# Attention weighing of the first four key tiles cut into two halves of the queries

## The reference, cut to what matters

```python
k = _layernorm(k, kln_w, kln_b)
q = _layernorm(q, qln_w, qln_b)
dot = jnp.einsum('bqhs,bkhs->bhqk', q, k) * scale
dot = jnp.where(causal, dot, -jnp.inf)
attn = jax.nn.softmax(dot, axis=-1)
out = jnp.einsum('bhqk,bkhs->bqhs', attn, v).reshape(b, t, e)
```

## Time and profile before

| what | value |
|---|---|
| median of three runs | 3361.61 us (3357.04 to 3369.52) |
| profiled execution, first to last instruction (span) | 3276.4 us |
| PE busy in the span | 2931.8 us (89%) |
| attention's 16 groups, 99.27 to 872.90 us | 773.63 us |
| PE busy in these | 682.38 us |
| granted TensorE clock in these | 0.72 |
| granted TensorE clock over the span | 0.891 |

### The profile page before, as it was taken

How to read it: one execution, slowest core, us unless ns; L and a number is a source line. 1 busy time by engine, 2 the same in 40 slices (tenths; PEclk the granted TensorE clock), 3 DMA queues, 4 the chain that set the end, 5 groups by cost and what they waited for, 6 DMA issues and landing times. The chain is left out here.

```text
span 3276.4 us, 55735 instructions
## 1 busy us (share of the span) xinstructions
PE 2931.8 (89%) x18642; PEld 1710.9 (52%) x18643; DVE 1759.5 (54%) x3206; ACT 1418.6 (43%) x2072; POOL 715.3 (22%) x865
## 2 busy tenths in 40 slices
PE   3898888988759995999999999999999999966997
PEld 1333343334348883555555555555555555545886
DVE  3555556555366674455555555554455544546666
ACT  1454455544534443444444444444444444424443
POOL 3031131311256331111111111111111111135632
PEclk7676777766769997999999999999999999976998
DMA  9000000000122215888888888888888888842222
GB/s 160 1 1 1 1 1 1 1 1 1 39 72 65 85 38 125 201 200 195 200 195 196 200 195 199 191 199 195 200 199 190 201 197 200 198 117 74 63 69 79
DMA packets 202915, 388.79 MB, mean 119 GB/s; under 512 B 44561, under 2 KB 117146, under 8 KB 198554
## 3 DMA queue, kind: packets, MB, share of 16 engines
q1 hardware_dynamic: 193562, 367.95, 48.8%
q0 software_dynamic: 9216, 19.02, 1.7%
HBM read 35.23 MB, written 31.75 MB: 20 GB/s over the span
## 5 line engine op out<-in xcount | busy, mean ns | idle before, releaser
L1911 DVE STREAM_TRANSPOSE m_turned<-m_sig 128x1024 f32<-128x1024 f32 x512 | 613.1, 1226 | 595.6 <-ACT m_sig L1824 575.1
L1824 ACT ACTIVATE m_sig<-m_f_ps 128x1024 f32<-128x1024 f32 x512 | 496.4, 1022 | 607.2 <-PE m_f_ps L1696 607.2
L743 DVE TENSOR_REDUCE a_maxima<-a_pair 128x2 f32<-128x1024 f32 (+3 forms) x384 | 354.7, 953 | 304.4 <-PE a_pair L416 240.2
L1709 PE MATMUL m_v_ps<-m_sig,m_tok 128*64 128x512 f32 x2048 | 496.1, 605 | 0.0
L1721 PE MATMUL m_v_ps<-m_sigT,m_tok 128*64 128x256 f32 x4096 | 465.6, 380 | 7.0 <-DMA m_sigT<-m_turned 6.9
L1696 PE MATMUL m_f_ps<-m_swap,m_own 64*128 64x512 f32 x1536 | 442.9, 421 | 11.0 <-DMA m_swap<-m_own 8.8
L1696 PE MATMUL m_f_ps<-m_own,m_swap 64*128 64x512 f32 x1536 | 442.9, 421 | 0.0
L561 ACT ACTIVATE a_prob<-a_pair 128x1024 f32<-128x1024 f32 (+3 forms) x384 | 303.3, 815 | 308.8 <-PE a_pair L429 299.8
L1721 PEld LDWEIGHTS m_v_ps<-m_sigT,m_tok 128*64 128x64 f32 x4096 | 293.8, 138 | 212.4 <-issue 69.1
L1696 PEld LDWEIGHTS m_f_ps<-m_swap,m_own 64*128 64x128 f32 x1536 | 270.9, 186 | 141.1 <-issue 86.0
L1848 POOL TENSOR_TENSOR m_own<-m_uv,m_own 128x1024 fp32r<-128x1024 f32 x64 | 152.0, 2375 | 841.0 <-ACT m_own L1809 841.0
(11 more groups left out here) (282 smaller groups left out, 4077.4 us busy)
## 6 DMA issues: line engine op xcount, KB each, us to landing
m_sigT<-m_turned SPq DMA_DIRECT2D x2048, 128.0 KB, 2.4
m_swap<-m_own SPq DMA_DIRECT2D x64, 512.0 KB, 4.4
m_swap<-m_own SPq DMA_DIRECT2D x64, 256.0 KB, 5.0
f_t_rows<-f_sent_rows SPq DMA_DIRECT2D x162, 65.0 KB, 1.8
f_sent_rows<-clear_rows SPq DMA_DIRECT2D x40, 260.0 KB
f_h<-back_rows SPq DMA_DIRECT2D x8, 512.0 KB, 5.0
f_norm_all<-back_rows SPq DMA_DIRECT2D x8, 512.0 KB, 5.6
back_rows<-f_y_rows,f_goes_to POOLq DMA_INDIRECT x160, 2.3
```

The source lines that it names most:

```text
L743: dve.tensor_reduce(maxima[:, qt, 2 * pair:2 * pair + 2, part], src, AX.X, ALU.max).then_inc(u.free(), 1)
L1709: mm = pe.matmul(v2_ps[h * RANK:(h + 1) * RANK, :], tok[p][:, j + s * SIDE, 0, :], sig[j % 2][s][:, h * HALF:(h + 1) * HALF], start=(j == ...
L1824: act.activation(sig[j % 2][s][:, :], f_ps[s][:, :], ACT.Sigmoid).then_inc(sig_ready, 1)
L1911: dve.transpose(turned[g][:, :, q, :, :], sig[j % 2][s][:, :].rearrange("p (t j a) -> p j t a", j=4, a=STACK)).then_inc(turn_ready, 1)
```

## The change

The weighing of tiles 0 to 3 is cut in two parts, (j, 0) for the queries up to 512 and (j, 1) for the rest. Part 1 stays where the whole weighing stood. Part 0 goes two score units ahead of it for tiles 0, 1 and 2 (behind units 5, 9, 13) and one ahead for tile 3 (behind unit 16). The matmuls, their operands and their waits are the same ones; tile 0's waits for `o_free` and `v_ready` go with its part 0, and the wait for the exponents is still for the tile's last unit, in both parts. Tiles 4 to 7 are weighed whole, as before.

```diff
+        WEIGH_AT = {}
+        for j in range(TILES - 1):
+            if j * P < HALF:
+                WEIGH_AT[LAST_OF[j + 1] - (2 if j < 3 else 1)] = (j, 0)
+            WEIGH_AT[LAST_OF[j + 1]] = (j, 1)
...
-                if i > LAST_OF[0] and i in LAST_OF:
-                    yield "weigh", LAST_OF.index(i) - 1
+                if i in WEIGH_AT:
+                    yield "weigh", WEIGH_AT[i]
...
-            def weigh(u, b, g, j, made):
+            def weigh(u, b, g, j, part, made):
 
                 G = GROUPS * b + g
                 u.wait_emptied(pe, made)
                 pe.wait_ge(kept, TILES * G + j + 1)
-                if j == 0:
+                if j == 0 and part == 0:
                     if not (isinstance(G, int) and G == 0):
                         pe.wait_ge(o_free, G)
                     if g == 0:
                         pe.wait_ge(v_ready, b + 1)
                 lo = j * P
-                for q0, q1 in ((lo, max(lo, HALF)), (max(lo, HALF), SEQ)):
-                    if q0 == q1:
-                        continue
-                    for h in range(GROUP):
-                        mm = pe.matmul(o_acc[h * STACK:(h + 1) * STACK, q0:q1], v1[:, j, g * GROUP + h, :],
-                                       prob[j % 2][:, h, q0:q1], start=(j == 0),
-                                       stop=(j == (3 if q1 == HALF else TILES - 1)))
+                q0, q1 = ((lo, HALF), (max(lo, HALF), SEQ))[part]
+                for h in range(GROUP):
+                    mm = pe.matmul(o_acc[h * STACK:(h + 1) * STACK, q0:q1], v1[:, j, g * GROUP + h, :],
+                                   prob[j % 2][:, h, q0:q1], start=(j == 0),
+                                   stop=(j == (3 if q1 == HALF else TILES - 1)))
```

More of the change, by code:

```diff
@@ L300, in sequence @@
                 if prev and i == 2:
-                    yield "weigh", TILES - 1
+                    yield "weigh", (TILES - 1, 1)
                 if prev and i == 4:
@@ L483, in group @@
                     elif what == "weigh":
-                        if n == TILES - 1:
-                            weigh(u, b - 1 if g == 0 else b, (g - 1) % GROUPS, n, last_of_prev)
+                        j, part = n
+                        if j == TILES - 1:
+                            weigh(u, b - 1 if g == 0 else b, (g - 1) % GROUPS, j, part, last_of_prev)
                         else:
-                            weigh(u, b, g, n, score_made[n])
+                            weigh(u, b, g, j, part, score_made[j])
                     elif what == "turn_out":
@@ L519, in _ @@
                 shifted = group(u, b, g, True, False, g < GROUPS - 1, shifted)
-            weigh(u, b, GROUPS - 1, TILES - 1, u.n)
+            weigh(u, b, GROUPS - 1, TILES - 1, 1, u.n)
             normed = turn_out(u, GROUPS * BATCH - 1)
```

## The result

The changed kernel takes 3385.48 us in the median of seven runs (3376.03 to 3394.81), the kernel before 3357.04 us in seven runs (3342.30 to 3369.52). The ratio is 1.0077, 95% interval 1.0058 to 1.0097: 28 us slower. The forecast was 3404 us, slower, with a range of 3328 to 3437.

What follows compares the result with a forecast made beforehand. TensorE was taken to bound where the clock is low. Terms 10.5 - 5.5 + 4.5 + 15.5 + 8 + 3 + 9 + 2 - 5 = +42 us took the span to 3318, the median to 3404 us; range 3328 to 3437.

Steps and rivals of the forecast that it cites:

- What bounds: Attention's sixteen groups: TensorE bounds where the clock is low; its work and its clock level can move the end.
- The halves don't lift the clock: Tiles 0 to 3: half blocks standing apart lose most clock rises; mean clock falls from 0.72 to about 0.65.
- Tiles 3, 4 and after: Lost high clock: +15.5 us at tile 3, +8 at tile 4, +3 until tiles 4 and 5 restore it.
- Tiles 0, 1, 2: Clock level at these weighings: +10.5 us at tile 0, -5.5 at tile 1, +4.5 at tile 2.
- -5 more for the three fourth groups: Tile 1: groups wholly low before gain a rise from part 0 beside `turn_out`, worth -5 us.
- lost rises: Tile 0: 9.5 of fifteen clock rises go because the halves stand apart, 1.1 us each, +10.5 us.
- Cuts +9: All 64 cut blocks: each cut costs TensorE between nothing and 0.2 us, taken as 0.14, +9 us.
- Waits +2, gain -5: Tile 0's earlier part 0 waits for ACT's copies, +2 us; half blocks shorten DVE and ACT gaps at high clock, -5.
- The held level: Rival: from tile 1's part 0 to tile 3 dense work holds the high clock; 3334 us, chance 0.17.
- Only moves: Rival: halves raise the clock as well, or rises only move; level terms nil, +6 us, 3368 us, chance 0.20.
- The new wait: Rival: tile 0's part 0 waits fully for ACT, starving the ring; another 16 to 30 us, 3425 us, chance 0.03.
- the rival without effect: Rival: level terms are nil since halves raise the clock too or rises only move; +6 us, 3368 us, chance 0.20.

Runs made afterwards that it cites:

- the doubled halves: The changed kernel with each half of tile 0's weighing issued twice: 3358.80 us, against 3387.46 for the changed kernel in the same session.
- the doubled scores: The changed kernel with score units 5 and 7 issued four times: 3324.25 us beside 3270.48 for the kernel before, ratio 1.0177.
- one changed number: The kernel before, uncut, with turn_out's eight transposes moved from behind unit 9 to behind unit 11: 3256.31 us against 3270.48, ratio 0.9947.

## Why the forecast was right, point by point

- **What bounds.** Right. Where the clock is low PE sets the pace. PE is busy for 22.7 us more with the same matmuls; some 9.5 of them are the cuts, which leaves some 13 for the clock. In the second profile of the changed kernel it is 33 us more, which leaves some 24.
- **The halves don't lift the clock.** Right, and shown by the doubled halves and the doubled scores. The mean clock of the groups fell less than forecast, from 0.72 to 0.69 and 0.68, where 0.65 had been named.
- **Tiles 3, 4 and after**, +15.5 +8 +3 = 26.5 us forecast: 28.4 and 27.9 us measured for units 16 to 22 in two profiles. The place is right: the stretch from tile 3 to tile 4 is low throughout in 7 and 8 groups where it was in 1. Agreement to 2 us is partly luck, for single profiles are compared here to within 10. And the forecast put the loss under tile 3; with tile 3 alone cut the level stays there, and it goes with the cut of tiles 1 and 2.
- **Tiles 0, 1, 2**, +9.5 us, with +6 for cuts, waits and gain, 15.5 in all: this is the sum's mis-sized part. The profiles show -15 and -12 us for units 4 to 16, against executions of the kernel before that were some 11 us above its median, so anything from -12 to about nil. One step that was off is tile 1's, "-5 more for the three fourth groups": in those, the high level now lasts from unit 6 to unit 12 or so, and units 4 to 12 take 4.3 us less each, -12.9. For tile 0, 9.5 lost rises had been forecast: a third or more of the units 8 and 9 is at the high level in 15 groups before and in 7 after, 8 lost, and 19 us of high level with them. Their price, 1.1 us each, can't be read by itself.
- **Cuts +9.** Right, and it can be read: 0.14 us at the high level and 0.16 at the low one, some 9.5 us over the 64 cuts. The working in the prediction (2.34 against 2.29) did not give that, since eight matmuls with 128 columns take 0.58 us and not the 0.47 put there; the 0.14 was a choice that came true. The Trainium skill (TensorEngine Tiling, Key Properties) speaks of a drain when the tiling mode changes, and a cut adds two such changes; whether it is they or the ends of the blocks that take the 0.14 to 0.16 us no run here separates.
- **Waits +2, gain -5.** PE's pauses shrink by 12 us in one profile and 15 in the other. Part of that is the lower clock, at which there is less to wait for. By the clocks of the runs cuts, waits and gain come to between -3 and +3 us together, where +6 had been taken.
- **Rivals.** The held level comes true in the fourth groups alone, three of sixteen; it makes some 8 of the 14 us between 42 and 28. "Only moves" is refuted by the clock. The new wait shows once in the whole profile (1.9 us for `o_acc`'s copy).
- **The number.** 3404 was reached from a median of 3361.6 of three runs; seven have 3357.0. What was forecast is +42 us, and +28 and +26 were measured. The range from 3328 to 3437 took in the rival without effect and half of the held level, so that the time lies in it says little.

What stays open: where the 11 us lie by which the profiled executions of the kernel before were above their median, why tiles 0 to 2 cost more together than apart, and what exactly the level follows. No run here separates how long a block must last from what it must hold.

## What to carry to other kernels

Where the granted clock moves between its levels inside a kernel that TensorE bounds, look at what stands ahead of each rise before rearranging; an order that spreads the dense blocks evenly between thin ones, which looks smoother, can cost more in clock than it saves in pauses, and putting two dense pieces side by side can be free time (here 14 us for one changed number). Test a suspicion of the clock by adding dense work: if the kernel gets faster, as here by 29 us, that speaks for the clock; if it doesn't, that does not speak against it (twice the clock rose here and the kernel was 5 and 12 us slower). Read the time of single executions against their own clock, and compare a trace only with traces whose execution lies as near its median.

## What was not expected of the hardware

- Adding 128 weighing matmuls to the changed kernel (256 in the profile) made it 29 us faster.
- Over 28 runs of one unchanged kernel on one chip the time, 3258 to 3280 us, goes with the mean granted clock with a correlation of -0.95.
- The same kernel takes 3267 us on one chip and 3362 us on another. The two expert stages make some 88 us of it (the kernels of this case differ in each of them by less than 6 us on one chip); the message stage takes 1651 to 1655 us on both. The cause was not looked for.
- PE can be busy nearly without a pause and stay at the low level. In the kernel before, 262.9 to 293.6 us, it was busy for 29.27 of 30.70 us at 0.50 throughout, for more than half of it with scores and maxima, which are matmuls on 32 rows, two at a time. The whole weighings of tiles 1, 2 and 3 stand in this stretch as well and did not raise the level, so a long block ahead is not always enough:

```profile
262.90:293.60 30.70, 29.27 (x148) 11.32 (x147) 20.42 (x28) 9.30 (x12) 2.66 (x7) 0.50 0.00 1
```
